# Attention's first round: where ScalarE's evictions stand among its conversions, and which engine converts head 1's A part

## What is computed

```python
Wh = jnp.einsum('nf,hfd->hnd', x, W)
e_src = jnp.einsum('hnd,hd->hn', Wh, a1)
e_dst = jnp.einsum('hnd,hd->hn', Wh, a2)
e = jax.nn.leaky_relu(e_src[:, :, None] + e_dst[:, None, :], ALPHA)
e = jnp.where(adj[None] > 0, e, NEG)
att = jax.nn.softmax(e, axis=-1)
h = jnp.einsum('hnm,hmd->hnd', att, Wh)
```

## Time and profile before

| | |
|---|---|
| median of 3 runs | 892.23 us |
| lowest and highest run | 890.35, 893.37 us |
| span of the profiled execution | 888.8 us |
| time of the profiled execution beyond its span | not given; the median is 3.4 us above the span |
| TensorE busy with products | 856.5 us, 96% of the span |
| VectorE, ScalarE, GpSimd busy | 690.8, 414.8, 276.1 us |
| attention, 16 rounds | from about 432 to about 816 us |

### The profile page before, as it was taken

The page is one execution under the profiler, slowest core; times in us unless marked ns, Lnnn a source line. Parts: engine busy times, 40 slices in busy tenths (PEclk is TensorE's granted clock), DMA queues, the critical chain, the costliest instruction groups (busy, mean ns, idle before and its releaser), DMA issues.

```text
span 888.8 us, 15240 instructions
## 1 busy us (share of the span) xinstructions
PE 856.5 (96%) x5145; PEld 751.4 (85%) x5145; DVE 690.8 (78%) x1187; ACT 414.8 (47%) x759; POOL 276.1 (31%) x293
## 2 busy tenths in 40 slices
PE   2999999999999999999779999999999999999998
PEld 2887888888888888778679999999999999999663
DVE  6788986556557775686999989999999999999722
ACT  3435433321111112345676666666666666775431
POOL 0000000000000000066736555555555555565222
PEclk9999999999999999999899999999999999999999
DMA  9969931603332331140051000000000032001043
GB/s 351 406 217 321 399 104 60 200 0 118 94 97 93 100 101 58 41 150 3 28 205 25 24 24 26 25 24 24 25 25 25 24 95 71 14 1 49 22 125 140
DMA packets 36117, 87.37 MB, mean 98 GB/s; under 512 B 7072, under 2 KB 7968, under 8 KB 36064
## 3 DMA queue, kind: packets, MB, share of 16 engines
q1 hardware_dynamic: 35024, 82.46, 27.3%
q0 software_dynamic: 1040, 4.26, 1.3%
HBM read 73.93 MB, written 12.78 MB: 98 GB/s over the span
## 4 chain that ended last, share of the span: by engine, by line
PE 86%; DVE 5%; DMA 3%; ACT 3%; issue 1%; POOL 1%; SPq 1%; POOLq 0%; DVEq 0%; ACTq 0%
PE bank L1550 27%; PE bank L1576 13%; PE bank L73 13%; PE bank L75 13%; PE bank L74 13%; PE bank L2008 3%; DMA l_h<-x 2%; DMA l_kept<-adj 1%; ACT l_mask L1323 1%; PE bank L1970 1%; DVE l_stats L224 1%; ACT s_hi L459 1%; PE bank L1991 1%; PE bank L2000 1%; DVE l_now L273 1%
## 5 line engine op out<-in xcount | busy, mean ns | idle before, releaser
L1203 DVE SCALAR_TENSOR_TENSOR l_q<-bank,neg_d,mask 128x512 fp32r<-128x512 f32 x512 | 338.7, 743 | 25.9 <-PE bank L1550 25.7
L1550 PE MATMUL bank<-l_parts,l_q 128*128 128x260 f32 x2048 | 251.7, 284 | 6.6 <-DVE l_q L1203 3.7
L1550 PEld LDWEIGHTS bank<-l_parts,l_q 128*128 128x128 f32 x2048 | 249.0, 190 | 7.1 <-issue 3.9
L73 PE MATMUL bank<-x_hi,s_hi 128*128 128x512 f32 x448 | 174.7, 390 | 1.2 <-DVE x_lo L264 0.9
L74 PE MATMUL bank<-x_lo,s_hi 128*128 128x512 f32 x448 | 174.3, 389 | 0.0
L75 PE MATMUL bank<-x_hi,s_lo 128*128 128x512 f32 x448 | 174.3, 389 | 0.0
L741 POOL TENSOR_TENSOR l_prod<-wh,l_a 128x512 f32<-128x512 f32 x30 | 36.2, 1227 | 391.8 <-ACT wh L713 391.8
L1323 ACT ACTIVATE l_mask<-mask 128x512 fp32r<-128x512 uint8 (+1 forms) x256 | 136.4, 620 | 0.9 <-PE bank L1576 0.8
L1576 PE MATMUL bank<-l_parts,l_mask 128*128 128x260 f32 x1024 | 128.7, 286 | 1.7 <-ACT l_o_q L1329 1.7
L1576 PEld LDWEIGHTS bank<-l_parts,l_mask 128*128 128x128 f32 x1024 | 127.0, 189 | 1.9 <-ACT l_o_q L1329 1.9
L73 PEld LDWEIGHTS bank<-x_hi,s_hi 128*128 128x128 f32 x448 | 84.1, 188 | 19.8 <-DVE x_lo L264 1.8
(11 more groups left out here) (174 smaller groups left out, 1078.9 us busy)
## 6 DMA issues: line engine op xcount, KB each, us to landing
rows<-adj_t SPq DMA_DIRECT2D x48, 512.0 KB, 3.9
l_now<-adj SPq DMA_DIRECT2D x16, 512.0 KB, 7.6
l_rows_k<-adj_t SPq DMA_DIRECT2D x16, 512.0 KB, 8.4
l_src<-e_rows SPq DMA_DIRECT2D x30, 256.0 KB, 3.2
l_kept<-adj SPq DMA_DIRECT2D x12, 512.0 KB, 13.2
wh_store<-wh POOLq DMA_DIRECT2D x1, 4160.0 KB, 15.8
l_h<-x SPq DMA_DIRECT2D x4, 1024.0 KB, 17.3
x<-x SPq DMA_DIRECT2D x1, 4096.0 KB, 13.4
```

The source lines that it names most:

```text
L73: pe.matmul(acc, hi, rhs_hi, start=first, stop=False, skip_group_check=True)
L1203: v.scalar_tensor_tensor(out=q[:, i, :], in0=bank[S_BANKS[hh]][:], scalar=neg_d[:, i, h:h + 1], in1=mask[:, i, cols], op0=ALU.is_ge, op1=A ...
L1550: return pe.matmul(bank[Q_BANKS[hh][t]][:, 0:PW], q[:, i, t * P:(t + 1) * P], parts[pair_slot][:, hh, i, :], start=i == 0, stop=i == T - 1)
```

## The change

VectorE: after head 0's 16 choices of round 0 it no longer makes the late arguments and the first low part at once. It makes them between head 1's choices: the first low part ahead of choice 2, the late arguments ahead of choice 4, and ahead of choice 8 it now also makes the conversion of head 1's A part (a copy that ScalarE made before) and then the second low part.

ScalarE: the conversion of the A part is gone. Head 1's C part is converted after four masks instead of eight; then come the four evictions of head 0, the other four masks and the eight after them, the factors B and D, `fill_src`, the evictions of the mask sums, and only then the wait for GpSimd's product and the conversion of it. In the other rounds the order is as before.

```diff
-                late_args(v)
-                second_rest(0)
-                choose(0, 0, 1, slice(0, QW), {G8: lambda: second_rest(1)})
+
+                def second_cut():
+                    v.wait_ge(late_whole_ready, 1)
+                    v.tensor_copy(parts[0][:, 1, :, A_HI], first_whole[3]).then_inc(second_hi, 1)
+                    second_rest(1)
+
+                choose(0, 0, 1, slice(0, QW), {2: lambda: second_rest(0), QUAD: lambda: late_args(v), G8: second_cut})
...
                 take_mask(0, 0, slice(0, QW))
-                take_mask(0, 1, slice(0, QW))
                 a.wait_ge(second_whole_ready, 1)
                 a.activation(parts[0][:, 1, :, C_HI], first_whole[2], ACT.Copy).then_inc(second_hi, 1)
-                late_factors(a)
                 take_q_sums(0, 0)
+                take_mask(0, 1, slice(0, QW))
...
                         if hp == 0 and r == 0:
-                            a.wait_ge(late_whole_ready, 1)
-                            a.activation(parts[0][:, 1, :, A_HI], first_whole[3], ACT.Copy).then_inc(second_hi, 1)
+                            late_factors(a)
                             fill_src(1, 0)
+                            take_m_sums(0)
                         if more:
                             a.wait_ge(whole_ready, r + 1)
                             a.sem_inc(held, 1)
                             a.activation(parts[(hp + 1) % 2][:, k, :, (A_HI, C_HI)[b]], whole[:], ACT.Copy
                                          ).then_inc(part_hi, 1)
-                        take_m_sums(r)
+                        if hp or r:
+                            take_m_sums(r)
```

## The result

The changed kernel takes **887.19 us** (median of 5 launches, 886.88 to 887.76); the median of the kernel before is now 892.33, of five launches that include the three of the table of before. The ratio is 0.9945, with a 95% interval of 0.9934 to 0.9956: 5.1 us, or 0.55%, faster. The forecast was 888.9 in a range of 887.0 to 891.7, with 0.63 on a gain of over 0.3%.

A forecast was written before the change was run, and what follows sets the result against it. TensorE was taken as the bound, with VectorE late next in round 1. TensorE alone would gain 3.67, less 0.30 for VectorE gives 3.37; 892.23 - 3.37 = 888.86, taken as 888.9, range 887.0 to 891.7.

The forecast's parts named there:

- The bound, and the two stalls: TensorE bounds; in round 0 it waits 1.7 us before the mask products and 2.9 us in head 1's, behind ScalarE's queue.
- Start of the mask products: Round 0's mask products on TensorE start at 446.00 instead of 446.58, VectorE's first low part blocked by GpSimd; gain 0.58.
- The rival of an unblocked low part: VectorE's first low part isn't held by GpSimd and ends at 445.12; gain 4.0, time 888.2; chance 0.12.
- VectorE as the next bound: VectorE's round 1 choices end at 467.96 and hold TensorE by 0.30, cutting the gain from 3.67 to 3.37.
- What was costed at nothing: Moved fill_src, SP's loads, the factors and ScalarE's next conversion and masks, with cover 0.5, cost no time.
- The store in flight: VectorE's copy and late arguments now run at 447 to 451 while GpSimd's store of wh is still in flight.
- the delay that the prediction took from the Trainium skill's page: The store of wh lands 1.2 later, delaying GpSimd's chain; gain 3.2; chance 0.14, shared with a slow copy.
- the slower rival: The store in flight holds VectorE's L888 up to 13.5 us; held for half, 895.6; chance 0.10.
- from the span to the median: The gain of 3.37 was subtracted from the median 892.23, which lies 3.4 above the profiled span of 888.8.
- The hole had been priced at its length: TensorE's idle stretch in round 0, 454.97 to 457.89, was counted as 2.92 us at a full granted clock.
- its lower end: Range's lower end 887.0: the time 888.2 with VectorE's first low part unblocked, with 1.2 given for the runs' scatter.

The follow-up runs named there:

- sums late: The changed kernel with ScalarE evicting round 0's mask sums after the next pair's conversion again, all else as changed; 889.00 us.
- sums first: The kernel before with one part of the change: in round 0 ScalarE evicts the mask sums before waiting for GpSimd's product; 889.59 us.
- last kernel: The changed kernel with GpSimd's store of wh first, its second head 1 product after VectorE's first low part, late arguments ahead of choice 6; 886.83 us.
- store-first kernel: The changed kernel with GpSimd's store of wh issued between its two products of head 1 instead of behind both; 889.69 us.
- ScalarE converts: The changed kernel with the A part's conversion given back to ScalarE, after its sixteen masks and before the factors; 890.99 us.
- the control: The kernel before with the first pair's four rounds written out on TensorE and no filling products; 892.04 us.
- store, then wait: The changed kernel with GpSimd's store of wh first and its second product of head 1 held until VectorE's first low part is done; 887.40 us.

## Why the prediction was right, and where it was off

**The bound, and the two stalls.** Right. The hole ahead of head 1's third product was ScalarE's order: undone alone it comes back (sums late), done alone it goes (sums first).

**Start of the mask products.** 0.58 was worked out, 0.57 measured from the first choice (14.59 to 14.02). The choice that was made there, that the low part is blocked by GpSimd's product, was the right one: it ended at 445.90 (445.78), 1.09 after the product, and TensorE began 0.23 later. With the low part one choice later it is not held and lasts 1.25. The rival of an unblocked low part was priced at a gain of 4.0: in the last kernel, where the low part lasts 1.24 and the arguments are out of the product's way, round 1's mask products start 4.01 earlier than before (37.28 for 41.29). The Trainium skill's page "SBUF — State Buffer", section "SBUF: two separate sides", says that whichever of a VectorE instruction with two SBUF inputs and a GpSimd instruction that reads SBUF starts first has the shared port pair for the whole instruction, and the other blocks. The changed kernel agrees (1.88 for 1.24); the store-first kernel doesn't by its recorded starts (VectorE's 444.00, GpSimd's 444.32, and VectorE waited). There the measurement decides: a start 0.32 us ahead was no protection.

**VectorE as the next bound.** Right, and nearly to a tenth: choices end 35.83 from the first one (35.96 was worked out: 467.96 on the clock of before, whose first choice is at 432.00), the wait was 0.34 (0.30), the conversion 0.70 (0.70), the late arguments 0.46 together (0.5). The doubled conversion moved the end one for one, and the part that was expected to win 3.1 without VectorE won 1.46 with it. What the prediction doesn't dwell on is where VectorE's time came from. From start to start the late arguments took 2.20 before (442.54 to 445.12 less a wait of 0.38) and take 0.38 after, since no product of GpSimd lies beneath them. That is 1.8 won, and it pays for the conversion (0.73) and the longer first low part (0.65); besides, two waits for ScalarE (0.38 and 1.04) are gone. The move of the late arguments was not tried alone.

**What was costed at nothing.** It cost nothing. ScalarE's masks were done at 451.66, 0.4 ahead of the last quarter of the mask products (0.5 was worked out); the evictions of round 1 followed L1381, which waited 0.59 for GpSimd, in time.

**The store in flight.** The first combination, which the store releases, started as far from the first choice as before (460.68 and 460.55, less 432.11 and 432.00: 28.57 and 28.55; 28.34 in the second profile of before), with the late arguments and the conversion now inside the store's flight. (The prediction calls it GpSimd's next product; the next one was L1496, at 454.42.) So the delay that the prediction took from the Trainium skill's page "SBUF — State Buffer", section "SBUF: two separate sides", didn't show here. Neither did its reverse, the slower rival: L888 took 0.21. The late arguments and the conversion came after the store's issue had ended (446.06), so these runs don't try what the Trainium skill describes, a copy on VectorE while GpSimd writes the descriptors.

**The step that was off: from the span to the median.** The sum was made against the span of one profile, and the gain was taken from the median. That took the profiled execution for a typical one with 3.4 us around it. What lies around the span is 1.8 (887.41 less 885.6), so this execution of before had taken about 890.6, 1.7 below the median of 892.33. A launch near the median (892.10, the second profile) pays for the hole twice: 2.9 us that TensorE stands still, and the half clock behind it. The hole had been priced at its length, at "a full granted clock", which was true of that launch and not of most. The term was short by 1.4 to 1.6 us, the filled hole's measure; with it the forecast would have been 887.3 to 887.5. That 887.19 lies in the range, 0.2 above its lower end, is luck: that end stood for an unblocked low part and the scatter of the runs, and the low part was blocked. The clock behind the hole had no term.

What stays open: why the clock falls behind the same 2.92 us in one launch and not in another was not settled, and no launch of before with a mean of 0.990 was profiled.

## What to carry to other kernels

Evictions that the bound engine waits for go ahead of everything in the queue that waits for a third engine; then look at once for the engine that is late next, because here it would have taken back more than half of the gain, and it took VectorE's other moves to keep it: with the conversion alone given back to ScalarE, all but 0.33 us of the 3.35 was lost in the trace, part of it to the clock. Price a hole of TensorE from several launches: it can cost its length and the clock behind it. When VectorE and GpSimd share a stretch, keep out from under GpSimd's products the VectorE instructions that wait for them here: the low part with its two SBUF inputs (1.88 and 3.40 for 1.24) and the late arguments (0.90 for 0.21). Moving one out of the way is worth nothing if the next one moves in.

## What the runs showed of the hardware that I had not expected

- The granted clock fell to half, for 3.4 us, behind holes of TensorE of 2.9 us (before, at 457.69 of its second profile), 2.7 us (store first, 448.86) and 1.8 us (ScalarE converts, 471.21), each beginning 0.4 us ahead of the hole's end to 1.2 us behind it. The products under it took 1.2 to 1.5 us longer. Not every hole had it: none did behind the 2.9 us of the first profile of before, nor behind the 1.64 us of "sums first, alone" and of "sums late". With the 2.9 us hole filled by 24 unread products, none of 11 launches had a mean clock under 0.993; of the control's 12 launches 6 had.
- A VectorE instruction with two SBUF inputs, recorded as starting 0.32 ahead of a GpSimd product, waited for all of it (3.40 for 1.24). The issue of the store beneath it doesn't hold it (1.24, store, then wait). Whether GpSimd's product has the port earlier than its recorded start was not tried.
